# The first 32 time steps of a gated recurrence as a row tile of their own, and another order of all work

## What is computed

```python
px = einsum('btc,dc->btd', layernorm(x), W_state) + b_state
g = sigmoid(einsum('btc,dc->btd', layernorm(x), W_gate) + b_gate)
def step(state, inp):            # over the 1024 time steps
    p_t, g_t = inp
    state = tanh(p_t + state)
    return (state, g_t * state)
x = x + layernorm(outs)
```

## Time and profile before

| | |
|---|---|
| time, median of 3 runs | 1593.18 us (1586.98 to 1593.67) |
| the profiled execution's own time | 1590.76 us |
| its span, first to last instruction | 1589.0 us |
| PE busy | 1393.2 us (88%) |
| DVE busy | 1096.9 us (69%) |
| ACT busy | 951.8 us (60%) |
| POOL busy | 317.6 us (20%) |
| mean granted clock of TensorE | 0.928 |

### The profile page before, as it was taken

The page is one execution under the profiler, slowest core; times in us unless marked ns, Lnnn a source line. Parts: engine busy times, 40 slices in busy tenths (PEclk is TensorE's granted clock), DMA queues, the critical chain, the costliest instruction groups (busy, mean ns, idle before and its releaser), DMA issues.

```text
span 1589.0 us, 33614 instructions
## 1 busy us (share of the span) xinstructions
PE 1393.2 (88%) x12320; PEld 1104.4 (70%) x12320; DVE 1096.9 (69%) x2884; ACT 951.8 (60%) x2090; POOL 317.6 (20%) x1146
## 2 busy tenths in 40 slices
PE   6905779999976799999999999999999899998997
PEld 3404668889863467778886577866787467875797
DVE  7867486655577967777888766787788667864242
ACT  2535465676555687777565846458544684567931
POOL 3343232223333323322332100001000100000000
PEclk9956579999985889999998999999999999999998
DMA  5584136855654445736666555574756556665443
GB/s 167 147 287 128 35 98 189 259 170 153 197 185 147 130 144 153 222 120 214 203 196 200 163 172 167 187 235 147 226 185 188 180 160 211 188 196 190 126 131 112
DMA packets 235572, 274.35 MB, mean 173 GB/s; under 512 B 36624, under 2 KB 158992, under 8 KB 235152
## 3 DMA queue, kind: packets, MB, share of 16 engines
q1 hardware_dynamic: 235408, 272.19, 56.2%
HBM read 229.98 MB, written 43.45 MB: 172 GB/s over the span
## 4 chain that ended last, share of the span: by engine, by line
PE 64%; DVE 10%; ACT 9%; DMA 7%; issue 4%; POOL 2%; SPq 2%; ACTq 0%; DVEq 0%; POOLq 0%
PE PS L1054 60%; ACT work L1008 3%; PE PS L1057 3%; DMA KT<-ktd 3%; POOL AD L1729 2%; ACT PX L940 2%; PE PS L1138 2%; SPq L862 1%; DVE mx L1528 1%; ACT work L1033 1%; DMA UU<-in_L_attn_x 1%; DMA work<-in_L_ffn_e_l 1%; DVE st L1340 1%; DMA ktd<-KTs 1%; DMA WB<-wlo_e_l 1%
## 5 line engine op out<-in xcount | busy, mean ns | idle before, releaser
L1729 POOL TENSOR_TENSOR AD<-PX 128x8 f32<-128x8 f32 x1023 | 247.7, 242 | 564.7 <-ACT PX L940 548.6
L940 ACT ACTIVATE PX<-AD 128x8 f32<-128x8 f32 x1023 | 219.3, 214 | 230.2 <-POOL AD L1729 227.6
L1008 ACT ACTIVATE work<-PS 128x1024 f32<-128x1024 f32 (+1 forms) x312 | 288.9, 960 | 85.9 <-PE PS L1054 84.7
L1528 DVE TENSOR_REDUCE mx<-PS 128x2 f32<-128x1024 f32 (+3 forms) x224 | 252.3, 1143 | 84.7 <-PE PS L1054 84.3
L1054 PE MATMUL PS<-work,vlx 128*32 128x256 f32 (+2 forms) x2816 | 240.8, 385 | 21.4 <-ACT work L1008 8.5
L1054 PE MATMUL PS<-EP,u_e_l 128*128 128x256 f32 x1024 | 193.7, 284 | 1.6 <-DVE EP L1388 1.4
L1736 POOL TENSOR_SCALAR_AFFINE_SELECT work<-work 128x512 f32<-128x512 f32 x96 | 65.0, 687 | 628.2 <-ACT work L1008 628.2
L1054 PE MATMUL PS<-WB,work 128*128 128x192 f32 x1024 | 182.6, 333 | 4.2 <-ACT work L1033 2.9
L1033 ACT ACTIVATE work<-PS 128x512 f32<-128x512 f32 x176 | 104.4, 597 | 127.6 <-PE PS L1054 125.9
L1054 PE MATMUL PS<-EP,WB 128*128 128x256 f32 x640 | 180.0, 281 | 0.0
L1054 PEld LDWEIGHTS PS<-WB,work 128*128 128x128 f32 x1024 | 167.5, 192 | 10.6 <-issue 6.2
(11 more groups left out here) (175 smaller groups left out, 2345.0 us busy)
## 6 DMA issues: line engine op xcount, KB each, us to landing
KT<-ktd SPq DMA_DIRECT2D x112, 512.0 KB, 4.7
WB<-wlo_e_l SPq DMA_DIRECT2D x160, 256.0 KB, 3.0
WB<-wlo_e_up SPq DMA_DIRECT2D x64, 256.0 KB, 3.1
WB<-wlo_e_w SPq DMA_DIRECT2D x64, 256.0 KB, 3.0
ktd<-KTs SPq DMA_DIRECT2D x112, 128.0 KB, 2.6
WB<-wdn_e_down SPq DMA_DIRECT2D x64, 192.0 KB, 2.5
KT<-ktd SPq DMA_DIRECT2D x48, 256.0 KB, 4.1
KT<-ktd SPq DMA_DIRECT2D x32, 384.0 KB, 4.2
```

What stands on the lines that cost most here:

```text
L940: eng.activation(cur, AD[n % 2], ACT.Tanh).then_inc(of(*key), 1)
L1008: eng.activation(pt[:, :, :, q0:L], two("sc", *a).rearrange("p a (l q) -> p a l q", l=2)[:, :, :, q0:L], ACT.Exp).then_inc(of(*key), 1)
L1528: eng.tensor_reduce(o, x, AX, ALU.max, negate=True).then_inc(of(*key), 1)
L1729: eng.tensor_tensor(AD[n % 2], PX[c % 2][:, :, :, t], PX[(n - 1) // L % 2][:, :, :, (n - 1) % L], ALU.add).then_inc(of(*key), 1)
```

## The change

The first row tile is cut in two. Time steps 0 to 31 of all four batches become a tile of 128 rows, batch by batch on the partitions, with operations of its own: `xinf` (four DMAs of 32 partitions), `hstf`, `hscf`, `htrf`, `hcpf`, `hpxf` (eight matmuls on 128 columns, state projection only) and `houtf`. Steps 0 to 31 of the recurrence wait for `houtf`. The other 96 time steps make three such tiles: `xin(0)` is four DMAs, `hst(0)` and `hsc(0,1..3)` work on three tiles, `hcp(0)` and `hpx0(0)` on 384 rows, and `hout0(0)` writes the steps 32 to 127. The gate projection `hpx1(0)` still runs once, on all 512 rows. `hst(0)` waits for `houtf`. All numbers of `START`, `AT` and `STAY` are new, so the order of all queues is another.

```diff
-STAY = {"pe": 24.2, "act": 5.7}
-START = (101.2, 162.6, 177.3, 239.6, 336.5, 416.5, 521.4, 595.3, 735.9, 806.3, 936.0, 1005.2, 1113.3, 1190.3, 1307.3, 1390.6)
-AT = {"piece": (-133.2, 84.2, 12.4, 109.4),
+STAY = {"pe": 28.6, "act": 9.4}
+START = (100.7, 166.4, 196.6, 254.9, 344.5, 419.3, 520.5, 597.3, 731.5, 806.3, 934.0, 1009.4, 1119.9, 1205.7, 1312.2, 1404.5)
+AT = {"piece": (-136.3, 203.2, -34.1, 173.6),
...
+    add("sp", ("xinf",), 1.4, -20.0, lat=3.5)
+    add("dve", ("hstf",), 2.3, -20.0, ("xinf",))
+    add("dve", ("hscf",), 0.42, -20.0, ("hstf",))
+    add("pe", ("htrf",), 0.25, -20.0, ("hscf",), ("ident",), mode="128",
+        take={"P1": (("hcpf",),), "xnT": (("hpx0", 0), ("hpx1", 0))}, lat=DRAIN)
+    add("dve", ("hcpf",), dve(256), -20.0, ("htrf",))
+    add("pe", ("hpxf",), 0.9, -20.0, ("hcpf",), ("wl", "x0"), mode="128", take={"P1": (("houtf",),)}, lat=DRAIN)
+    add("dve", ("houtf",), 0.62, -20.0, ("hpxf",), ("wl", "bs"))
...
-        add("dve", ("hst", n), 3.75, d, ("xin", n))
+        add("dve", ("hst", n), 3.75 if n else 3.4, d, ("xin", n), *([] if n else [("houtf",)]))
...
-        px = [("hout0", 2 * c + t // 128)] if c < 2 else [("pxl", c)]
+        px = [("houtf",)] if n < 32 else [("hout0", 2 * c + t // 128)] if c < 2 else [("pxl", c)]
...
+                elif kind == "xinf" or key == ("xin", 0):
+                    for b in range(B):
+                        x = A["L0_attn_x"][b, 0:128, :].rearrange("(i t) d -> t i d", t=32)
+                        i = slice(0, 1) if kind == "xinf" else slice(1, 4)
+                        eng.dma_start(half(0)[32 * b:32 * b + 32, i, :], x[:, i, :]).then_inc(of(*key), 16)
...
+                elif kind == "hpxf":
+                    pe.wait_ge(*done("wl", "x0"))
+                    pe.wait_ge(*done("hcpf"))
+                    for m in range(2):
+                        for kc in range(2):
+                            ins = mm(one(*key)[:, 128 * m:128 * m + 128], wx[:, kc, 128 * m:128 * m + 128], normed(0)[:, kc, 0:128],
+                                     kc == 0, kc == 1)
+                    ins.then_inc(of(*key), 1)
...
+                elif kind == "houtf":
+                    v.wait_ge(*done("wl", "bs"))
+                    v.wait_ge(*done("hpxf"))
+                    for m in range(2):
+                        src = one("hpxf")[:, 128 * m:128 * m + 128].rearrange("p (b t) -> p b t", b=B)
+                        ins = eng.tensor_scalar(PX[0][:, m, :, 0:32], src, bx[:, m:m + 1], None, ALU.add)
+                    ins.then_inc(of(*key), 1)
```

More of the change, by code:

```diff
@@ new lines @@
+STAY = {"pe": 28.6, "act": 9.4}
+START = (100.7, 166.4, 196.6, 254.9, 344.5, 419.3, 520.5, 597.3, 731.5, 806.3, 934.0, 1009.4, 1119.9, 1205.7, 1312.2, 1404.5)
+AT = {"piece": (-136.3, 203.2, -34.1, 173.6),
+      "post": (166.8, 83.6, -37.7, -36.8),
+      "prep": (-14.4, -64.9, -47.8, 38.7),
+      "value": (-121.3, 2.2, -155.4, -124.5),
+      "key": (-134.3, -72.1, 52.0, -70.4),
+      "query": (-57.2, -45.8, -83.5, -34.3),
+      "max": (-79.8, -42.0, -50.6, -41.1),
+      "maxima": (1.6, -1.7, 10.0, 41.5),
+      "bound": (107.4, 11.0, 122.0, -4.0),
+      "score": (43.4, 43.8, 31.3, 50.8),
+      "scores": (17.9, 9.8, 16.5, 14.9),
+      "av": (43.5, -26.4, 10.9, 24.6),
+      "merge": (34.1, -32.0, -8.1, 4.2),
+      "out": (-205.7, -19.7, -168.4, -53.1),
+      "gate": (-121.5, -171.3, -104.2, 66.0),
+      "l1": (1.6, 254.8, 190.7, 207.2),
+      "e0up": (162.4, 157.3, -15.9, 330.6),
+      "l2": (251.3, 338.2, 208.6, 225.9),
+      "e0dn": (342.1, 358.4, 447.6, 8.0),
+      "e1": (282.2, 263.3, 257.4, 326.1),
+      "l3": (197.0, 277.0, 218.0, 408.5),
+      "e3dn": (164.9, 319.1, 226.2, 298.9),
+      "e1dn": (339.6, 338.5, 336.0, 343.2),
+      "l4": (234.0, 268.5, 43.0, 315.6),
+      "e3up": (302.1, 337.0, 278.4, 297.3),
+      "e3out": (216.0, 262.0, 322.4, 502.6),
+      "fin": (244.3, 207.2, 242.3, 457.4)}
@@ L299, in arrange @@
             else:
-                add("dve", ("hout0", n), 1.4, d, ("hpx0", n), ("cbx", 0))
+                add("dve", ("hout0", n), 1.4, d, ("hpx0", n), ("wl", "bs"))
             if staged:
@@ L935, in _ @@
                     if n == 0:
-                        act.wait_ge(*done("hout0", 0))
+                        act.wait_ge(*done("houtf"))
                         eng.activation(cur, cur, ACT.Tanh).then_inc(of(*key), 1)
@@ L949, in _ @@
                     act.wait_ge(*done("hpx1", n))
-                    eng.activation(dst[:, m, 128 * b:128 * b + 128], two("hpx1", n)[:, m, 128 * b:128 * b + 128], ACT.Tanh,
-                                   bias=bx[:, 2 + m:3 + m], scale=0.5).then_inc(of(*key), 1)
+                    eng.activation(dst, src, ACT.Tanh, bias=bx[:, 2 + m:3 + m], scale=0.5).then_inc(of(*key), 1)
                 elif kind == "pcp":
@@ L1066, in _ @@
                         pe.wait_ge(*x)
-                if kind == "htr":
+                if kind == "htrf":
+                    pe.wait_ge(*done("ident"))
+                    pe.wait_ge(*done("hscf"))
+                    for kc in range(2):
+                        ins = tr(one(*key)[:, 128 * kc:128 * kc + 128], half(0)[:, 0, 128 * kc:128 * kc + 128])
+                    ins.then_inc(of(*key), 1)
+                elif kind == "htr":
                     n, i = a
-                    ps = two("htr", n, 0)
+                    first = 0 if n else 1
+                    ps, col = two("htr", n, first), 128 * (i - first)
                     pe.wait_ge(*done("ident"))
@@ L1079, in _ @@
                     pe.wait_ge(*done("hcp", n))
-                    xn = xnT[place[("htr", n, 0), "xnT"]]
+                    if n == 0:
+                        pe.wait_ge(*done("hcpf"))
+                    done_before = 0 if n or gate else 128
                     for m in range(2):
```

96 lines of the change are left out of this document (50 added, 46 removed).

## The result

| | before | changed |
|---|---|---|
| time, median of 4 runs each | 1593.29 us (1586.98 to 1593.67) | 1612.31 us (1609.77 to 1616.63) |
| profiled execution, its span | 1590.76, 1589.0 us | 1612.67, 1610.9 us |
| mean granted clock of TensorE | 0.928 | 0.921 |

The ratio is 1.0132, with a 95% interval from 1.0098 to 1.0165: the changed kernel is 1.3% slower. The forecast was 0.3% faster, with a range up to 1600 us. The time lies outside it.

A forecast was written before the change was run, and what follows sets the result against it. TensorE was taken as starved at 23.80 to 250 and 450 to 600 us, itself the bound at 250 to 416. Gains 4 + 2 - 1 = 5 us less gave 1588 us; range 1577 to 1600, the forecast's own 1582 to 1592.

The forecast's parts named there:

- Start of the recurrence: Input stage: with the small first tile the first tanh comes at about 15.8 us, 8.0 us earlier (6 to 10).
- Lead at step 31: ScalarE waits up to 2.2 us at the first gate activation behind tanh 30; step 127 ends at 92.2 us, 9.6 earlier.
- ptr(0): End of input stage: it waits for the last gate tile's store, so starts at 99 us, 4.6 us earlier, not 9.6.
- pln(0): Start of unit 0: with 5 weight-piece pairs ahead instead of 16, it starts near 101 us, 8.1 us earlier.
- Weight pieces: VectorE in unit 0: pieces moved later take 10.7 us, 4 exposed, plus 1.7 among maxima; 2.4 of 8.1 us left.
- TensorE's work up to `ptr(4)` is the same set in both queues, and full: 4 us it stays.: Dense stretch, 250 to 416 us: the 4 us lead (0 to 8) carries through, ptr(4) near 415 us.
- Second starved stretch: From ptr(4) to unit 6's first scores: five more operations, some 6.4 us, fill idle time; taken as 2 us gained.
- The rest: Behind the first scores of unit 6: TensorE's work otherwise the same, shape changes nothing, table loads 1 us lost.
- Table loads: ScalarE: 126 instead of 114 at 1.28 us, 15.4 us more work, ten behind the last step; 1 us taken.
- Rival 3: Score stretches of units 12 to 15: added table loads on ScalarE's path, 1604.6 us, or 1597 with half; chance 0.13.
- Rivals 1, 2 and 4: 1: lead carries in full, 1579 us, 0.16; 2: lead used up, 1592, 0.22; 4: start no earlier, about 1592, 0.04.
- the two signs of being wrong: ptr(4) not 2 to 6 us earlier, or the stretches from 1200 us on taking over 5 us longer.

The follow-up runs named there:

- h4: Changed kernel, but for 13 of 19 weight pieces the low-half subtraction makes only 16 of 256 columns, leaving out part of the computation; 1.0155 of the kernel before.
- f2: Changed kernel's first part up to ptr(4), then the old orders with the old banks and buffers; 1.0054 of the kernel before.
- e2: Changed kernel's orders up to ptr(4), then the old orders, with banks chosen by the planner; 1.0124 of the kernel before.
- g1: Changed kernel with fin(9) moved on VectorE from ahead of avc(10,0) to behind mgd(10,0), all banks and buffers kept; 1.0149 of the kernel before.
- g0: Changed kernel as it is, measured again beside three others on one chip; 1.0154 of the kernel before.
- e3: Changed kernel's orders up to the first scores of unit 6, then the old orders, with banks chosen by the planner; 1.0091 of the kernel before.
- e4: Changed kernel's orders up to ptr(12), then the old orders, with banks chosen by the planner; 1.0165 of the kernel before.
- g2: As g1, with three more VectorE operations, pu(8), pu(11) and pu(12), moved one or two places later; 1.0133 of the kernel before.
- e1: Tile and changed orders up to unit 0's first expert matmul, then the old orders, with banks chosen by the planner; 1.0084 of the kernel before.
- f1: As e1, but from unit 0's first expert matmul on every operation also gets its old bank and buffer; 0.9973 of the kernel before.
- g3: As f1 up to ptr(4), then the changed kernel's orders and banks; 1.0132 of the kernel before.
- h1: As f1 up to ptr(12), then the changed kernel's orders and all but two of its banks; 1.0071 of the kernel before.
- h2: As h1, but with the switch to the changed kernel's orders at ptr(8); 1.0241 of the kernel before.
- j1: f1 with ten expert matmul groups of unit 11 moved from between unit 12's scores to ahead of them, banks kept; 1.0113 of the kernel before.
- j2: f1 with four Gelus or exponentials moved past each other on ScalarE, 106 table loads instead of 114; 1.0029 of the kernel before.
- f3: Kernel before in code, tile and orders, with e1's banks and buffers from unit 0's first expert matmul on; 1.0074 of the kernel before.
- h3: Kernel before plus six tiny Gelus between exponentials in units 13 to 15, so 12 more table loads; 1.0085 of the kernel before.

## Why the prediction was wrong

- **Start of the recurrence, right.** First tanh at 15.39 us (15.8 forecast); `hpxf` 2.05 us (2.0), `houtf` 0.61 us (0.6).
- **Lead at step 31, right.** ScalarE waits 0.82 us ahead of the first gate activation (up to 2.2), and step 127 ends at 92.17 us (92.2).
- **`ptr(0)`, right, by two errors.** 98.97 us, released by the last gate store (99). But the input stage's last projection ends at 91.0 us, not 85.6. The sum took 58.6 us for a stretch that is 59.5 us by its own rows, and from 22 us on TensorE waits three times, 5.6 us in all, for VectorE's copies. The last gate activation ends at 95.1 us (95) because it follows that projection, not because of its place behind the steps. That the two errors cancel is luck.
- **`pln(0)`, nearly right.** 101.9 us (101): 7.0 us earlier than before, where 8.1 were forecast.
- **Weight pieces, the sum right, its reason too large.** The first experts of unit 0 start 4.4 us earlier than before (4 forecast). h4 shows that the pieces expose less than I took.
- **"TensorE's work up to `ptr(4)` is the same set in both queues, and full: 4 us it stays." Wrong, the first step that failed.** In the changed kernel `ptr(4)` is at 423.2 us, not 415. TensorE idles 6.3 us more on the way, above all for two transfers that hadn't landed (4.03 and 2.69 us). Equal sets say nothing of whether each operation's data are there when its turn comes. Seven other profiles of kernels with its orders up to here have `ptr(4)` 1.9 to 8.3 us late (f2, e2, g1, g0, e3, e4, g2). With the tile and the old orders from unit 0's experts on it is 4.6 us early to 4.5 us late in seven profiles, +0.2 us in the mean (e1, f1, g3, h1, h2, j1, j2), against +5.1 in the eight with the new ones. So the new order costs some 5 us up to here, and the 4 us of lead can't be seen at `ptr(4)` with either.
- **Second starved stretch, right in direction, more than forecast.** From `ptr(4)` to the first scores of unit 6 it takes 1.6 us longer, with 6.4 us more work done: 4.8 us gained (2 forecast).
- **"The rest. TensorE's list of work is otherwise the same ... nothing." Wrong, and this is the loss.** I compared totals (matmuls, shape changes, table loads) of the 1000 us behind unit 6 and gave them 1 us. What the runs show in its place: with the new orders behind `ptr(4)` the tile kernel is 1.6% slower than with the old ones (g3 against f1), and TensorE loses 11 to 13 us more between unit 10's scores and some 8 us more between unit 8's, in idle time and lower clock. That it is the expert work missing there is likely by j1, where moving it alone cost 22 us. Which bank each matmul gets is a second thing that no total shows. It is worth 0.7% in f3 and 1.1% between e1 and f1; whether it has a part in the changed kernel's own loss is open.
- **Table loads.** Their number and length were right (126, 1.28 us as in the earlier trace rows). The Trainium skill, ScalarE: Activation LUTs, section What ACT_TABLE_LOAD costs, has 2.66 us for a switch. The traces stand against it: in h3 one load runs from 1293.60 us to 1294.88 us, the activation behind it starts at 1294.89 us, and the next load follows that one at 1295.10 us, with no gap for a drain. The twelve loads made that kernel 13.6 us slower, 1.1 us each. Of the changed kernel's loads, the 1 us I took isn't contradicted.
- **Rivals.** Rival 3 gave 1604.6 us, the nearest, by a mechanism that is real (h3), but of which the changed kernel's trace shows nothing. Rivals 1, 2 and 4 dealt with the start, where nothing was decided. The rival that was missing: the new orders themselves are worse. Of the two signs of being wrong that were named, `ptr(4)` came true; the stretches behind 1200 us did not take longer (+27.1 us at 1187 us and +23.4 us at 1491 us in the table).

The tile with the orders of the start alone gives by f1 the 4 us that the forecast had for the start (interval 1.6 to 7 us). The 5 us less that were forecast for the whole would have been right for it, without the new orders behind.

## What to carry to other kernels

- Where several engines feed TensorE over a stretch (scores, exponentials, maxima), independent matmuls standing between kept it busy and at the higher clock (f1 against j1: clock 0.96 and 0.81). Look at them unit by unit before and after a change of order; a total hides a unit that has none. The count is a hint, not a price: unit 9 lost a third of its groups and nothing else.
- An order and its bank assignment are one thing. Where only the order was kept, 0.7 and 1.1% went. When a change is tested, pin both, or the test measures the planner.
- A wait that is seen is not the price of what it waits for: ask what would have been late next (here a 5.7 us load of keys), and test it by taking the wait away before a total is built on it.

## What was not expected of the hardware

- Twelve table loads of 1.28 us between exponentials cost 13.6 us (h3), though TensorE was busy for 253 of the 265 us from 1280 us on in the kernel before.
- The same orders and banks up to `ptr(4)` put it at -4.6, -3.1, +1.1, +2.4, +3.4 and +4.5 us against the kernel before in six profiled kernels (j2, h1, j1, h2, f1, g3). A shift of under some 9 us at one point of one profile is no evidence by itself; the 4 us of the tile come from the ratio of many runs.
- The 512 KB load of keys for `sc(10,1,0)` takes 5.7 us from issue to landing in the changed kernel and in g1, where TensorE waits for it; the median of such loads is 4.7 us.
